# The values' products of a window-attention kernel: 64 by 64 tiles for each image instead of 128 by 64 tiles over two

## The reference

```python
# window attention: 8 x 8 windows of N = 64 tokens, 4 heads of hd = 16
qkv = ln_c(x) @ w_qkv.T
attn = softmax(q @ k.T * hd**-0.5 + bias)
out = (attn @ v) @ w_proj.T + b_proj
x = x + out
# experts: 8 experts, the best 2 of each token
t = x + sum_k top_p[k] * (ln_t(x) @ expert_w[top_i[k]] + expert_b[top_i[k]])
```

## Time and profile before

| | |
|---|---|
| median of three runs | 1152.46 us (1150.5 to 1160.61) |
| span of the profiled execution | 1154.0 us |
| granted TensorE clock, mean | 0.985 of full speed |
| TensorE matmul (PE) busy | 1050.4 us, 91% |
| TensorE weight load (PEld) busy | 597.6 us, 52% |
| VectorE (DVE) | 875.0 us, 76% |
| ScalarE (ACT) | 748.4 us, 65% |
| GpSimd (POOL) | 463.1 us, 40% |
| DMA | 189.61 MB, 164 GB/s |

### The profile page before, as it was taken

One profiled execution on the slowest core, in us unless ns is written; L12 is line 12 of the kernel. 1 busy time (PEld: TensorE's weight loads), 2 busy tenths in 40 slices (PEclk: granted clock), 3 DMA queues, 4 the chain that ended last, 5 costly groups with the idle time before them and its releaser, 6 DMA issues.

```text
span 1154.0 us, 39247 instructions
## 1 busy us (share of the span) xinstructions
PE 1050.4 (91%) x16886; PEld 597.6 (52%) x16886; DVE 875.0 (76%) x1355; ACT 748.4 (65%) x1218; POOL 463.1 (40%) x509
## 2 busy tenths in 40 slices
PE   4798899999999999999999999999999999988857
PEld 3455555555555555555555544555555555554312
DVE  4567678878777777787777877778887787787874
ACT  1688577767776767677766666777776677665410
POOL 1013443444344334434434443443434434443550
PEclk9999999999999999999999999999999999999878
DMA  6016467878777668877776787677778876747885
GB/s 188 2 39 138 106 148 173 202 184 193 177 168 170 171 166 192 194 172 170 181 168 166 187 187 181 155 177 180 177 176 193 195 172 164 171 112 178 190 179 130
DMA packets 48872, 189.61 MB, mean 164 GB/s; under 512 B 10494, under 2 KB 10750, under 8 KB 32572
## 3 DMA queue, kind: packets, MB, share of 16 engines
q1 hardware_dynamic: 48700, 187.10, 68.3%
HBM read 151.15 MB, written 18.87 MB: 147 GB/s over the span
## 4 chain that ended last, share of the span: by engine, by line
PE 59%; DVE 19%; POOL 7%; DMA 6%; issue 6%; ACT 2%; SPq 0%; POOLq 0%; DVEq 0%; ACTq 0%
PE bank L568 8%; PE bank L689 8%; PE bank L585 8%; PE bank L546 5%; PE bank L559 5%; DMA gz<-gates_dram 5%; DVE Ls L1827 5%; PE bank L602 4%; PE bank L609 4%; DVE probs L1728 3%; DVE mx L1721 3%; PE bank L621 3%; PE bank L516 3%; POOL vr L1527 3%; PE bank L630 2%
## 5 line engine op out<-in xcount | busy, mean ns | idle before, releaser
L689 PE MATMUL bank<-gz,wex 64*64 64x512 f32 x2048 | 259.4, 612 | 9.0 <-DVE gz L1743 9.0
L1536 POOL TENSOR_TENSOR gz<-gz,tt 128x1024 f32<-128x1024 f32 x94 | 229.2, 2440 | 63.9 <-DMA gz<-gates_dram 63.9
L1117 ACT ACTIVATE pt<-bank 128x512 f32<-128x512 f32 x256 | 151.7, 593 | 119.7 <-PE bank L585 118.8
L1728 DVE TENSOR_TENSOR probs<-bank,mx 128x1024 f32<-128x1024 f32 x128 | 156.7, 1224 | 94.7 <-PE bank L585 91.6
L1743 DVE TENSOR_TENSOR gz<-gz,tt 128x1024 f32<-128x1024 f32 x156 | 196.9, 1280 | 5.0 <-DMA gz<-gates_dram 5.0
L1497 POOL TENSOR_TENSOR tt<-prj,xs 128x512 f32<-128x512 f32 x64 | 82.4, 1308 | 291.3 <-ACT prj L1134 291.3
L1721 DVE TENSOR_REDUCE mx<-bank 128x16 f32<-128x1024 f32 x128 | 156.0, 1219 | 34.4 <-PE bank L568 33.5
L585 PE MATMUL bank<-cst,probs 128*128 128x128 f32 x1024 | 165.7, 285 | 3.0 <-ACT pt L1117 2.5
L585 PEld LDWEIGHTS bank<-cst,probs 128*128 128x128 f32 x1024 | 111.7, 141 | 87.8 <-issue 67.5
L568 PE MATMUL bank<-km,qs 32*64 32x128 f32 x4096 | 143.8, 275 | 4.8 <-issue 4.8
L689 PEld LDWEIGHTS bank<-gz,wex 64*64 64x64 f32 x2048 | 74.2, 135 | 125.6 <-issue 104.2
(11 more groups left out here) (122 smaller groups left out, 1480.0 us busy)
## 6 DMA issues: line engine op xcount, KB each, us to landing
gz<-gates_dram SPq DMA_DIRECT2D x250, 512.0 KB, 8.7
xs<-in_x SPq DMA_DIRECT2D x32, 512.0 KB, 9.0
tx<-tt SPq DMA_DIRECT2D x128, 128.0 KB, 2.8
out<-ob SPq DMA_DIRECT2D x128, 128.0 KB, 9.9
gz<-in_rel SPq DMA_DIRECT2D x1, 2048.0 KB, 9.5
gates_dram<-gt_rs SPq DMA_DIRECT2D x32, 64.0 KB
cst<-in_consts SPq DMA_DIRECT2D x1, 359.0 KB, 3.0
tt<-in_weights SPq DMA_DIRECT2D x4, 64.0 KB, 5.0
```

The lines of the kernel that those rows point to most:

```text
L689: last = mm(bank[64 * x:64 * x + 64, Y_BANK + a, :], wex[64 * a:64 * a + 64, e, :], gz[64 * a:64 * a + 64, s.pair(e)[1], e % 2, x * CH:(x ...
L1117: af(pt[g % 2][:, u % 2, :, :, :, :].rearrange("p j h x q -> p (j h x q)"), bank[:, PT_BANK, :], ACT.Copy).then_inc(pt_ready, 1)
L1536: tt_(gz[:, k, e % 2, :], gz[:, k, e % 2, :], tt[s.buf(4)][:, :], op=ALU.mult).then_inc(z_pool, 1)
L1728: tt_(probs[g % 2][:, :, :, :].rearrange("p h w (m k) -> p (h w m) k", k=N), two_banks(S_BANK).rearrange("p (c k) -> p c k", k=N), mx[g % ...
```

## The change

`value_rows` takes each image by itself. A matmul takes the 64 rows of one image of a window as the stationary operand and the 32 columns of this image and parity as the moving one, so no zero is multiplied. The row tile is the image's, the column tile the parity's: four 64 by 64 tiles take turns. The result goes to bank `PRE + a`, at 32 columns for each window, both halves of the strip behind one another. A strip has 64 such matmuls in place of 32. `vbd` gets its image as the outer dimension, so that `move_v` still copies two banks in the order in which they lie; the slices that `values` reads are 32 neighbouring elements as before.

```diff
-        vbd = sb("vbd", [P, 2 * CW, 4, 2, HD])
+        vbd = sb("vbd", [P, 2, 2 * CW, 2, 2, HD])
...
                 for x in range(2):
                     for w in range(CW):
-                        for m in range(2):
-                            last = mm(bank[64 * m:64 * m + 64, PRE + x, 64 * w:64 * w + 64].rearrange(
-                                "p (a g d) -> p a g d", a=2, d=HD), xr[s.buf(2)][:, x, w, :], wv[:, m], start=True, stop=True)
+                        at = 2 * HD * (CW * x + w)
+                        for a in range(2):
+                            for m in range(2):
+                                last = mm(bank[64 * m:64 * m + 64, PRE + a, at:at + 2 * HD].rearrange(
+                                    "p (g d) -> p g d", d=HD), xr[s.buf(2)][64 * a:64 * a + 64, x, w, :],
+                                    wv[64 * a:64 * a + 64, m, a], start=True, stop=True)
                 last.then_inc(v_full, 1)
...
-                           vbd[:, CW * (r // 2) + w, 2 * a + r % 2, :, :].rearrange("p m d -> p (m d)"),
+                           vbd[:, a, CW * (r // 2) + w, r % 2, :, :].rearrange("p m d -> p (m d)"),
...
-                af(vbd[rows, :, :, m, :].rearrange("p w g d -> p (w g) d"),
+                af(vbd[rows, :, :, :, m, :].rearrange("p a w g d -> p (a w g) d"),
                    two_banks(PRE)[rows].rearrange("p (v d) -> p v d", d=HD), ACT.Copy).then_inc(v_ready, 1)
...
-                nc.gpsimd.memset(vbd[:, :, :, :, :], 0.0).then_inc(zeroed, 1)
+                nc.gpsimd.memset(vbd[:, :, :, :, :, :], 0.0).then_inc(zeroed, 1)
```

## The result

The changed kernel takes 1195.65 us (median of four runs, 1189.32 to 1198.82), the kernel before beside it 1156.53 us: a ratio of 1.0336, 95% interval 1.028 to 1.0393. It is slower, as forecast, but by 39 us where I had 16, and its time lies 6 us above my range. The profiled execution has a span of 1191.2 us, 37.2 more than before.

A forecast was written before the change was run, and what follows sets the result against it. TensorE was taken to bound the kernel: 1154.0 - 4 (shorter rounds) + 20 (pauses at instruction packet ends) = 1170 us for the profiled execution, 1168 us against the median; range 1147 to 1190 us.

The forecast's parts named there:

- The bound, the rounds, the tiles: Values' block (line 546): TensorE sets the time, 32 rounds as before, and four 64 by 64 tiles load side by side.
- Row tiles in turn: Rival: in the values' block two images' loads of a column tile can't overlap, 56 us more, 1208 us; chance 0.06.
- the rival without cost of packets: Rival: instruction fetch runs far enough ahead, earlier pauses are late packets behind experts' transfers, nothing lost, 1148 us; chance 0.26.
- so 0.13 us, and 32 strips give 4 us: Values' block: a round takes 54 to 55 ns in place of 59, saving 4 us over the run.
- The block's pauses: TensorE waits for packets of 256 instructions in or shortly behind the values' block: 23 us, taken as 20.
- the table of the prediction: Pause by the block instruction where a packet ends: behind it 1.5 us at 0, 0.4 at 64; before it 1.1 at 192, 1.5 at 256.
- The pauses there are ... move to other places, since packets end elsewhere. I count them as they are: Existing pauses in lines 602 and 568, 8.6 + 4.8 us, move elsewhere but keep their size.
- Part of it may fall into waits of PE that are there anyway: Part of the block's 23 us of pauses falls into existing waits, such as the shifted scores' 17.1 us; 20 us taken.
- R: Time PE needs for each 256 instructions, from one packet's end to the next's: taken as 3.46 us, at least 2.65.

The follow-up runs named there:

- e2: Changed kernel with all 128 rows in each product, 64 matmuls a strip on two tiles in place of four: 1217.41 us, ratio 1.0517.
- e7: Changed kernel with 97 satisfied waits a strip in 25 strips and 108 once at the start, packet ends at the block's instruction 100: 1153.13 us.
- e9: The kernel of e7 with 234 in place of 108 waits at the start, packet ends at instruction 230 of each block: 1281.59 us.
- e12: Kernel before with the spread gates' loads cut to a quarter of their elements from the third strip on: 1136.8 us, ratio 0.9843.
- e4: Kernel before with 64 tiny products (128 more TensorE instructions) a strip ahead of the queries' products: 1197.04 us, ratio 1.0336.
- e5: Changed kernel padded with tiny products to 1280 instructions a strip in 25 strips, packet ends at the block's instruction 100: 1204.51 us, ratio 1.0402.

## Why the prediction was wrong in size

**The bound, the rounds, the tiles: right.** Unpaused blocks take 2.0 us to the next line, as before. 64 by 64 tiles load side by side (e2 is the proof: without them 1.8 us more). Row tiles in turn, the rival of 1208 us, is refuted although the time came near it; so is the rival without cost of packets, by e7 against e9. Its premise on the pauses of before, late packets behind the transfers, holds nearly whole (e12); that the block then loses nothing doesn't. The Trainium skill (TensorE: Matmul & The Clock Gate, section "Wait — 56ns, not 53.3ns?") has 25 ns as the least between two matmuls; the 126 products 14.7 ns apart disagree over a whole block.

**"so 0.13 us, and 32 strips give 4 us": wrong, 0.** Steady strips without a pause take 32.5 to 32.7 us in both kernels, pauses and clock taken off. The 59 ns of a round are not stream and load in each other's way: e2, with half of the stream, has 58. Line 482's 54.0 ns was the nearest row, but a bf16 one of another shape; why it is shorter is open.

**The block's pauses: mechanism and place right, size nearly.** I had 23 us before absorption. Measured are 27.3 less the 2.3 there were. The places follow the table of the prediction: in strips 4 to 28 no end within the block's first 136 instructions pauses, all 13 from 137 to 253 pause for 0.5 to 2.4 us (I had 0 at 128, 1.1 at 192, 1.5 at 256), then six of seven for 0.6 to 1.1 us up to 323, and none from 342 to the end of this stretch (I had 0.4 at 320 and 0 at 384).

**"The pauses there are ... move to other places, since packets end elsewhere. I count them as they are": this step failed, by 11 us.** Behind the first 350 instructions pauses rose from 15.3 to 26.1 us. In before, nearly all the ends that pause lie between instructions 738 and 862 from the block. In after, where the same products are 128 further on, nearly all lie between 862 and 1002: what would be 734 to 874. The stretch is 140 instructions in place of 124, and in the rest of the strip 19 ends pause in place of 14, at the same 1.1 us each; two or three more in the 350 ahead of it make up the difference. e12 shows what I had left out: these pauses come from the transfers, nearly all of them. At these ends the next packet's first byte came some 5.6 us after the end before, in both kernels, where it came 1.2 us after it around the block of after. That their number depends on where 128 more instructions put the ends against the transfers is argued; e4 shows that instructions added elsewhere also raise them (15.3 to some 33 us there). Why this many fall there is not settled; that another alignment gives fewer than before, e7 shows.

**A term was missing: the clock, 6 us.** I priced a pause at its own length. A pause of 2 us, or a cluster of idle times, can be followed by 5 us at the lower level, and needn't be. In after this is 6 of the 37 us.

**"Part of it may fall into waits of PE that are there anyway": half right.** In the steady strips next to nothing was absorbed. At the beginning and end of the run it was 4 to 5 us by the difference of the sums, not of the block's 23 alone.

The sum as it was: 1154.0 + 0 (for -4) + 25 (for 20) + 11 (for 0) + 6 (for 0) - 5 = 1191, against 1170. The 5 us absorbed are what is left over. The direction came true for the reason given, the block's pauses; the largest misses are the 11 and the 6 us, which I had put at nothing.

**R.** I took 3.46 us from a quiet stretch and used it in busy ones. With light traffic the block's pauses are 14.9 us, less than its 23; with full traffic 27.3. So 3.46 sat between the two, and was no bound of either. Nor is R one number. Taken from one packet end to the next where the second one pauses, it is 2.9 to 4.7 us around the block of after (median 3.9), but 7.4 to 11.2 us in the rest of its strips (median 8.2) and 7.2 to 10.6 in before (outer tenths left out). So the pauses of the earlier trace rows, which I left as they were, come from an R more than twice as long as mine. The Trainium skill (Runtime: NRT & Kernel Launch, section "Instruction fetch mechanics") calls a crossing mostly hidden. It is: 101 of 150 show no pause. The other 49 are the whole effect, and with e9's alignment nearly two a strip.

## What to carry to other kernels

Where an engine's waits end in "issue" inside a block that waits for nobody, count its instructions: if they recur at every 256th, the price of a change is how many instructions it puts into how little time. Splitting matmuls into more, smaller ones can keep the engine's pace and lose by the instructions alone. Before such a change is given up, the alignment can be set: make a strip a multiple of 256 instructions with a few satisfied waits in slow stretches, and move the ends out of the dense ones. In the steady strips e7 against e9 is 103 us by nothing else. Which places are good has to be tried: e5, with the ends as many instructions behind the block's start as e7, pauses in every strip.

A pause can have two prices, its length and the clock behind it.

## What the runs showed of the hardware

- TensorE stands still at every 256th instruction of its stream when the next packet is late, and goes on some 2.3 to 3.2 us after that packet's first byte (49 pauses of after, median 2.8, the outer tenths left out).
- After three of four idle times of 2 us or more in the steady strips of after the granted clock fell to 0.50; behind the one at 601 us PE worked for 5 us at it.
- 64-row, 64-column weight loads on four tiles keep 59 ns for a round (14.7 ns apart), 128-row ones on two 58 to 59 (29.0 and 29.5 ns apart): twice the loads in the same time.
- Data transfers delay the first byte of an instruction packet: median 2.4 us after the packet end before in after, 1.2 us with a quarter of the gates' traffic.
- Satisfied waits are nearly free for TensorE in groups of 7 and not in groups of 16: 225 of them a strip cost 291 us, 121.5 of it waits ahead of the experts' products; 97 of them cost 0.3 us a strip.
